# Moving the second norm's transposes and the gate's product behind the scores of their slots in a decoder layer

## The reference

```python
x = _layernorm(x + _L0_attn_ref(x, Wq, Wk, Wv))                       # 16 heads, one key and value head
x = _layernorm(x + _L0_xattn_ref(x, ctx, ctx, mask, W1, b1, W2, b2))  # the second norm
x = _layernorm(x + _L0_ffn_ref(x, Wg, W1, b1, Wo, bo))                # the third
# in _L0_ffn_ref: gate_logits = x @ Wg.T; softmax; top 2 of 8; g = a * sigmoid(b); out += (g @ Wo.T + bo) * comb
```

## Time and profile before

| | us |
|---|---|
| median of 3 runs | 1400.23 |
| lowest and highest of the 3 | 1399.9, 1410.04 |
| profiled execution | 1407.59 |
| its span, first to last instruction | 1405.2 |

### The profile page before, as it was taken

How to read it: one execution, slowest core, us unless ns; L and a number is a source line. 1 busy time by engine, 2 the same in 40 slices (tenths; PEclk the granted TensorE clock), 3 DMA queues, 4 the chain that set the end, 5 groups by cost and what they waited for, 6 DMA issues and landing times.

```text
span 1405.2 us, 30425 instructions
## 1 busy us (share of the span) xinstructions
PE 1272.8 (91%) x7734; PEld 901.7 (64%) x7735; DVE 1105.5 (79%) x3115; ACT 746.3 (53%) x1740; POOL 637.3 (45%) x917
## 2 busy tenths in 40 slices
PE   6988999999989999999998759899999999997997
PEld 4443555556555555555554447688888888877997
DVE  1566798888988889898897656678888888876997
ACT  1235677787777877777776412233222322323555
POOL 3011245554555545455454523665465565551333
PEclk7998999999999999999999759999999999998999
DMA  6647497897987879777574784888788788877885
GB/s 187 174 94 142 100 213 177 219 213 201 219 178 195 183 205 213 167 175 162 136 145 174 259 297 83 129 135 131 123 138 136 122 137 135 131 107 240 281 274 179
DMA packets 194871, 242.73 MB, mean 173 GB/s; under 512 B 21712, under 2 KB 144592, under 8 KB 190544
## 3 DMA queue, kind: packets, MB, share of 16 engines
q1 hardware_dynamic: 159392, 153.70, 45.8%
q0 software_dynamic: 26128, 54.94, 22.8%
q10 hardware_dynamic: 9248, 32.86, 7.1%
HBM read 142.46 MB, written 120.24 MB: 187 GB/s over the span
## 4 chain that ended last, share of the span: by engine, by line
PE 68%; DVE 9%; issue 7%; DMA 7%; ACT 4%; POOL 3%; SPq 2%; DVEq 0%; ACTq 0%; POOLq 0%
PE psHb L1445 7%; PE psHb L1441 6%; PE psHb L1442 6%; PE psO L644 6%; PE psS L751 5%; PE psB L673 4%; PE psHa L1441 4%; PE psHa L1442 4%; PE psHa L1445 4%; PE psT L761 4%; DVE negmax L1065 3%; DMA qstack<-q_parts 2%; PE psHa L1498 2%; PE psX L1465 2%; PE psA L633 2%
## 5 line engine op out<-in xcount | busy, mean ns | idle before, releaser
L1065 DVE TENSOR_REDUCE negmax<-psS 128x2 f32<-128x512 f32 x512 | 350.5, 687 | 101.2 <-PE psS L751 83.4
L904 ACT ACTIVATE probs<-psT 128x512 f32<-128x512 f32 x512 | 303.2, 598 | 164.3 <-PE psT L761 149.1
L1523 ACT ACTIVATE sig<-hb 128x512 f32<-128x512 f32 x135 | 85.4, 633 | 297.1 <-DVE hb L1598 243.7
L1406 POOL DMA_INDIRECT g_rows<-g,slot x135 | 211.9, 1569 | 37.3 <-issue 34.8
L751 PE MATMUL psS<-kstack,qstack 96*128 96x256 bf16 x1024 | 195.9, 274 | 30.9 <-DVE kstack L1163 12.0
L761 PE MATMUL psT<-qstack,kstack 99*128 99x512 bf16 x512 | 194.9, 383 | 4.5 <-ACT probs L904 4.5
L751 PEld LDWEIGHTS psS<-kstack,qstack 96*128 96x128 bf16 x1024 | 93.6, 104 | 90.3 <-DVE negmax L1065 24.9
L503 POOL DMA_INDIRECT lists<-x,slots x128 | 128.6, 1005 | 33.9 <-issue 30.1
L644 PE MATMUL psO<-probs,vaug 128*32 128x512 f32 x1024 | 139.0, 615 | 0.4 <-ACT probs L904 0.4
L1607 DVE SCALAR_TENSOR_TENSOR g<-g,xe,sig 128x512 f32<-128x512 f32 x135 | 101.6, 752 | 26.1 <-ACT sig L1523 11.7
L1441 PE MATMUL psHb<-w_hi,xet_hi 128*128 x270 | 118.6, 439 | 0.0
(11 more groups left out here) (210 smaller groups left out, 2799.4 us busy)
## 6 DMA issues: line engine op xcount, KB each, us to landing
qstack<-q_parts SPq DMA_DIRECT2D x192, 128.0 KB
g_rows<-zero_rows ACTq DMA_DIRECT2D x20, 1024.0 KB, 6.8
xe<-lists SPq DMA_DIRECT2D x135, 132.5 KB
rows<-g_rows SPq DMA_DIRECT2D x32, 512.0 KB, 5.0
q_parts<-qpart SPq DMA_DIRECT2D x32, 384.0 KB
sums<-x SPq DMA_DIRECT2D x32, 264.0 KB
x2in<-sums SPq DMA_DIRECT2D x32, 264.0 KB, 3.4
xt<-in_x_t SPq DMA_DIRECT2D x32, 256.0 KB
```

What stands on the lines that cost most here:

```text
L904: nc.scalar.activation(probs[:, u % PT, :], psT[:, u % 2, :], ACT.Exp, scale=SELF_SCALE).then_inc(sm["exp_done"], 1)
L1065: v.tensor_reduce(negmax[:, b1.s2, 2 * hp:2 * hp + 2, c], psS[:, u % 2, :].rearrange("p (h k) -> p h k", h=2), AX.X, ALU.max, negate=True) ...
L1406: pool.indirect_dma_start(out=dram["g_rows"], out_offset=bass.IndirectOffsetOnAxis(ap=slot[:, o.s4:o.s4 + 1], axis=0), in_=g[:, o.s4], in_ ...
```

## The change

Two groups on TensorE move from the head of their slots to the end of the same slots, behind the slot's scores and (in slot 5) values: the second norm's transposes in slot 5 and the gate's product in slot 7. On VectorE the copy of the logits moves from slot 7 to slot 8, where it stands behind that slot's maximum; in the draining steps it also comes to stand behind `drain_slot`, which in slot 8 makes the statistics of the first norm. Nothing is added or removed, and no buffer or semaphore changes.

```diff
--- before.py
+++ after.py
@@ -681,28 +681,12 @@
                             last = mm(psA[:, c * SC:(c + 1) * SC], x1t[:, b5.s2, k, c * P:(c + 1) * P],
                                       keymap[:, k, bass.ds(b5.n * SC, SC)], start=k == 0, stop=k == DC - 1)
                     last.then_inc(sm["cross_scored"], 1)
-                if u == 5 and active(b6):
-                    wait(pe, "x2_ready", done(b6))
-                    bank_read(bank_b, t, "x2_transposed")
-                    for c in range(QC):
-                        for k in range(DC):
-                            last = nc.tensor.transpose(psB[:, k * S + c * P:k * S + (c + 1) * P],
-                                                       x2[:, b6.s2, c, k * P:(k + 1) * P], ident[:, :])
-                    last.then_inc(sm["x2_transposed"], 1)
                 if u == 6 and active(b2):
                     wait(pe, "m_split", done(b2))
                     bank_read(bank_a, t, "m_transposed")
                     nc.tensor.transpose(psA[0:MROWS * NH * QC, 0:P // 2].bitcast(BF16),
                                         mpart[:, b2.s2].rearrange("p m h c -> p (m h c)"), ident_b[:, :]
                                         ).then_inc(sm["m_transposed"], 1)
-                if u == 7 and active(b6):
-                    wait(pe, "x2t_copied", done(b6))
-                    bank_read(bank_b, t, "gate_scored")
-                    for c in range(QC):
-                        for k in range(DC):
-                            last = mm(psB[:, c * E:(c + 1) * E], x2t[:, b6.s2, k, c * P:(c + 1) * P], wg[:, k, :],
-                                      start=k == 0, stop=k == DC - 1)
-                    last.then_inc(sm["gate_scored"], 1)
                 if u == (0 if draining(t) else 8) and active(b4):
                     att_transpose(t, 0)
                 if u == (4 if draining(t) else 10) and active(b4):
@@ -762,6 +746,22 @@
                        start=True, stop=True).then_inc(sm["scored"], 1)
                     if u % 4 == 1 and u > 4:
                         pv(b3, u // 4 - 1)
+                if u == 5 and active(b6):
+                    wait(pe, "x2_ready", done(b6))
+                    bank_read(bank_b, t, "x2_transposed")
+                    for c in range(QC):
+                        for k in range(DC):
+                            last = nc.tensor.transpose(psB[:, k * S + c * P:k * S + (c + 1) * P],
+                                                       x2[:, b6.s2, c, k * P:(k + 1) * P], ident[:, :])
+                    last.then_inc(sm["x2_transposed"], 1)
+                if u == 7 and active(b6):
+                    wait(pe, "x2t_copied", done(b6))
+                    bank_read(bank_b, t, "gate_scored")
+                    for c in range(QC):
+                        for k in range(DC):
+                            last = mm(psB[:, c * E:(c + 1) * E], x2t[:, b6.s2, k, c * P:(c + 1) * P], wg[:, k, :],
+                                      start=k == 0, stop=k == DC - 1)
+                    last.then_inc(sm["gate_scored"], 1)
             if t.fixed and t.n == 0:
                 fold_projections()
             for g, part in context_parts(t, UNITS):
@@ -1102,7 +1102,7 @@
                     wait(dve, "score_link", done(b5))
                     v.tensor_reduce(cnegmax[:, b5.s2], cscore[:, b5.s2], AX.X, ALU.max, negate=True
                                     ).then_inc(sm["cross_masked"], 1)
-                if u == 7 and active(b6):
+                if u == 8 and active(b6):
                     wait(dve, "gate_scored", done(b6))
                     wait(dve, "gate_exp", done(b6.back(2)))
                     v.tensor_copy(logits[:, b6.s2], psB[:, 0:QC * E].rearrange("p (c e) -> p c e", c=QC)
```

## The result

The changed kernel takes 1436.37 us (median of 4, 1429.99 to 1444.41), the kernel before 1400.43 beside it. The ratio is 1.0238 with an interval of 1.0196 to 1.0281: **slower by 2.4%**, where the prediction said 1394.8 and left 0.04 for slower by over 1%. The profiled execution took 1444.41 (span 1441.9), 36.8 more than the one of before.

What follows compares the result with a forecast made beforehand. TensorE and VectorE were taken as nearly full, with TensorE's order setting the step. 1.03 - 0.79 = 0.24 us a step, 27 steps: 6.5 - 0.8 - 0.3 = 5.4 us off 1400.23, so 1394.8; range 1390 to 1403.

Steps and rivals of the forecast that it cites:

- The old wait: Slot 5: TensorE waits 1.03 us a step ahead of the second norm's transposes; the change removes it.
- tight place: Slot 7: its scores have 0.02 us of room behind slot 5's maximum, the gate 0.18 behind `x2t`.
- The place and the releaser of the new wait: Slot 9: TensorE waits ahead of line 714 until VectorE, in order, has read the logits behind slot 8's maximum.
- The size of the new wait: Slot 9: TensorE waits 0.79 us anew, counting 0.42 from slot 8's scores to its maximum.
- nothing on SP or POOL comes later: Transfer queues: with the copy earlier, line 417 and the loads into `qstack` come earlier, and nothing there later.
- The clock: Attention stage, steady part: granted clock 1.00 in the profile of the kernel before; no term for a lower clock.
- Two small terms: Slots 7 to 9: release from logits to transposes about 0.05 us, gate's product 0.81, within a gain of 0.24.
- No new wait: Slot 9: the logits read is free or not needed; 27.8 us off, 1372.4, or about 1386; chance 0.05.
- VectorE late: Slot 8: VectorE reaches its maximum late; loss from 0.68 us a step on, 1408.8 at 1.0; chance 0.08.
- All given back: Slots 5, 9 and 0: the two waits cancel or the `qstack` transfer fills the gain; 1400; chance 0.15.

Runs made afterwards that it cites:

- e7: Changed kernel with the first half of GpSimd's dispatch held back behind slot 9's transposes of the cross probabilities: 1403.51 us, 1.0002 of the kernel before.
- e5: Changed kernel with 12 small matmuls without use put on TensorE ahead of slot 9's wait for the logits: 1417.05 us, 1.0117 of the kernel before.
- e11: Changed kernel with logits read in slot 7 again and the dispatch's first half held behind slot 9's transposes: 1401.36 us, 0.9982 of the kernel before.
- e9: Changed kernel with logits read in slot 7 again and the dispatch's first half held behind ScalarE's slot 10 copy: 1388.21 us, 0.9892 of the kernel before.
- e10: Kernel before with only the dispatch's first half held back behind slot 9's transposes of the cross probabilities: 1407.11 us, ratio 1.0009.
- e2: Kernel before with only the read of the logits moved from slot 7 to slot 8: 1431.18 us, ratio 1.0206.

## Why the prediction was wrong

**The old wait: right.** The 1.03 us ahead of the second norm's transposes is gone, and neither tight place cost anything: no row of slot 7's scores or of the gate has idle time ahead of it.

**The place and the releaser of the new wait: right.** TensorE waits ahead of line 714 (now 698), the logits end that wait, and they follow the maximum by 0.61 (406.44 - 405.84). VectorE did not slip the read ahead.

**The size of the new wait: this step failed.** The prediction had the maximum of slot 8 start 0.42 us behind its scores, from a row of slot 5, and took that as true of every slot and step. In after it is 0.43 in step 12 and 1.03 in step 16, and the longer one is the rule. The wait that was put at 0.79 was then 1.50. What the runs put in its place: TensorE's signals in that stretch of the step come late, by up to 0.62 us, while GpSimd issues a dispatch beside SyncE's transfers, and this lateness already lay in before, where the attention's transposes raised theirs at 9.69 and not at 9.38. The prediction counted "nothing on SP or POOL comes later" as all there was to say of these queues. It did not ask what comes at the same time as a signal that had just become critical. By e7 against e5 this costs about 1.2% (1.0117 against 1.0002).

**The clock: a step that was missing.** The prediction made its sum at a granted clock of 1.00, as before had it, and priced a wait at its own length. In after fifteen of 25 steps pay about 1.5 us more behind it (22.7 together against e5). By e5 that is another 1.2% (1.0238 against 1.0117).

The Trainium skill, "TensorE: Matmul & The Clock Gate" (section on what is actually happening), says that the lower clock is the state without activity and that work releases it. The trace agrees in kind: the 0.50 stands behind the wait, and the fill in e5 brings 1.00 back.

**Two small terms.** Even in a step with its signal on time the gain was 0.09 (21.82 to 21.73) and not 0.24: the release from the logits to line 698 took 314.37 - 314.23 = 0.14 and not the 0.05 that the prediction took without a row, and the gate's product 0.89 (311.67 to 312.56) and not 0.81. In e7, where all else is as the prediction had it, the gain of 0.08 a step can't be measured: 1.0002.

**The rivals.** No new wait fell at once. "VectorE late" had the right side and the right place, a late start of slot 8's maximum, and its arithmetic holds for the wait: a maximum that starts 0.60 later than forecast costs 0.60 - 0.24 = 0.36 a step, 27 x 0.36 = 9.7 us over 1400.2, about 1410. The step with the late signal at 2.4 GHz is 22.33 - 21.82 = 0.51 longer than before's: the 0.15 more are the two small terms, and 27 x 0.51 gives about 1414. What lies above that is the clock. But VectorE was not late: it stood idle 1.38 us ahead of that maximum. The test that the prediction named ("a maximum of slot 8 that starts well over 0.42 after its scores") came out, for a cause that was not on the list. "All given back" is what e7 shows without the dispatch beside it.

**What stays open.** Why a dispatch holds TensorE's signals back was not settled, nor whether it is GpSimd's work on it or the data that it moves. It does not do it always: at 8.23 us beside SyncE's transfers it does, at 10.70 in e11 too, a little at 12.54 in e9, while at 10.27 and 11.62 in e7 no signal is late. Which transfer it has to meet besides line 417, the store of the queries or their loads, was not tried apart. Nor was it settled why four steps of after escape. Why the clock fell in fifteen steps and not in six others is open too. The length of the wait does not decide it: the fifteen waits are 0.99 to 1.35 us by their rows, the six 1.29 to 1.35. The other 36.8 - 31.3 = 5.5 us of the profiled execution lie behind the 25 steps: from step 31 to the first matmul of the second stage it is 133.7 us in place of 126.6, ahead of step 6 it is 1.7 less, and the second stage takes 566 us in both. With the fill of e5 that stretch takes 126.1, so there, too, the clock is the likely cause.

## What to carry to other kernels

When a read that frees a buffer is moved behind another instruction, its wait inherits everything that this instruction waits for, with every disturbance of it; so look at the spread of that releaser over many steps and at the transfers that run beside it, not at one typical row. A lateness that nobody waits for is in the trace all the same: consumers of different engines that start within 0.04 us of each other, though their producers lay 0.22 apart, are its mark. And price a wait of a TensorE that is nearly full with the clock behind it: a dozen matmuls without use in the wait tell whether it is the waiting or the clock that costs.

## What the runs showed of the hardware

TensorE's signals can be held back, several at once, for 0.1 to 0.9 us while its matmuls start on time; they then come 0.03 to 0.04 us apart. Holding back GpSimd's indirect transfers made those of slot 8 punctual in after (e7), in before (e10) and in e9; in step 6, which has no dispatch, they are on time as well; and moving the dispatch can move the lateness (e11: 0.3 to 0.9 us, about 11 us into a step).

A wait of 0.99 to 1.35 us by its row, once a step, was followed by the 1.2 GHz level in fifteen of after's 25 steps (the eight value matmuls of step 16 took 1.87 us in place of 1.00), while waits of 1.29 to 1.35 in six other steps were not. In e7 waits of 0.95 and 0.91 were followed by it in steps 6 and 7, while two waits of 0.87 and 0.91 in one step of e2 were not.
